# Expert results stored in sorted order and fetched by row number, in place of a scatter to token order

## What is computed

```python
x = x + gnn(layernorm(x), adj, W, a)         # attention inside each block of 128 tokens
x = x + ffn(layernorm(x), gate_w, gate_b, w1, w2, w3)

# gnn, for each block
Wh = h @ W.T; e = leaky_relu((Wh @ a1)[:, None] + (Wh @ a2)[None, :])
out = softmax(where(adj > 0, e, -9e15)) @ Wh

# ffn: 16 experts, hidden 256, each token goes to its best two
probs = softmax(x @ gate_w + gate_b); top2 = top_k(probs, 2); gates = top2 / sum(top2)
out = sum over the two of  gate * ((silu(x @ w1[e]) * (x @ w2[e])) @ w3[e])
```

## Time and profile before

| | |
|---|---|
| timed, median of 3 | 522.09 us (520.78 to 522.9) |
| profiled execution, span from first to last instruction | 661.6 us |
| its own time | recorded only as that span |
| TensorE busy | 409.6 us, 62% |
| VectorE busy | 250.0 us, 38% |
| GpSimd busy | 316.4 us, 48% |
| mean granted TensorE clock | 0.804 |

### The profile page before, as it was taken

One profiled execution on the slowest core, in us unless ns is written; L12 is line 12 of the kernel. 1 busy time (PEld: TensorE's weight loads), 2 busy tenths in 40 slices (PEclk: granted clock), 3 DMA queues, 4 the chain that ended last, 5 costly groups with the idle time before them and its releaser, 6 DMA issues.

```text
span 661.6 us, 10734 instructions
## 1 busy us (share of the span) xinstructions
PE 409.6 (62%) x2857; PEld 372.2 (56%) x2860; DVE 250.0 (38%) x915; ACT 194.3 (29%) x516; POOL 316.4 (48%) x340
## 2 busy tenths in 40 slices
PE   3787863675520313773563788697877888878700
PEld 2576753554520313672462778687777888777700
DVE  2898898654356001120110122221221234343328
ACT  1687760454310101220120133322322333232200
POOL 3123321657477771557357444444444445643530
PEclk9999995679555575985677689898997989997855
DMA  3999992696131312351342455555555579777347
GB/s 105 225 234 240 248 255 63 148 185 159 58 126 52 100 68 95 133 196 68 119 155 80 159 195 210 177 198 194 188 191 196 191 259 312 246 255 263 130 167 242
DMA packets 126058, 113.88 MB, mean 172 GB/s; under 512 B 10704, under 2 KB 100944, under 8 KB 126032
## 3 DMA queue, kind: packets, MB, share of 16 engines
q1 hardware_dynamic: 116816, 94.64, 49.2%
q0 software_dynamic: 9216, 18.96, 8.2%
HBM read 33.72 MB, written 33.70 MB: 102 GB/s over the span
## 4 chain that ended last, share of the span: by engine, by line
PE 36%; issue 23%; DVE 14%; another core or an unknown queue 9%; DMA 7%; ACT 5%; POOL 2%; SPq 2%; DVEq 1%; ACTq 0%; POOLq 0%
PE bank L475 21%; PE bank L484 8%; PE bank L384 4%; DMA shared<-in_adj_dram 3%; DMA w_t<-W 2%; DVE prob L815 2%; ACT em L590 2%; DVE stats L635 1%; DVE h L645 1%; DVE X L698 1%; ACT h L536 1%; POOL token_rows L924 1%; PE bank L428 1%; PE bank L430 1%
## 5 line engine op out<-in xcount | busy, mean ns | idle before, releaser
L924 POOL DMA_INDIRECT token_rows<-shared,DEST x160 | 154.1, 963 | 179.4 <-ACT shared L596 127.4
L475 PE MATMUL bank<-xT,w_t 128*128 128x128 f32 x1280 | 196.2, 298 | 49.2 <-issue 27.5
L475 PEld LDWEIGHTS bank<-xT,w_t 128*128 128x128 f32 x1280 | 176.0, 211 | 56.0 <-issue 41.0
L815 DVE TENSOR_TENSOR prob<-em,bank 128x256 f32<-128x256 f32 x160 | 66.6, 421 | 316.9 <-ACT em L590 214.0
L916 POOL DMA_INDIRECT sorted_rows<-H,ROW x128 | 125.6, 981 | 53.0 <-issue 37.4
L484 PE MATMUL bank<-W,prob 128*128 x640 | 109.9, 298 | 61.5 <-DVE prob L815 33.4
L590 ACT ACTIVATE em<-bank 128x256 f32<-128x256 f32 x160 | 60.6, 387 | 275.2 <-PE bank L475 135.6
L484 PEld LDWEIGHTS bank<-W,prob 128*128 128x128 f32 x640 | 92.8, 209 | 70.6 <-issue 70.5
L904 POOL TENSOR_TENSOR rstd<-var_eps,half_neg 128x4 f32<-128x4 f32 x32 | 32.3, 1022 | 82.8 <-DVE var_eps L651 82.8
L384 PE MATMUL bank<-ident,xs_t 128*128 128x128 f32 x160 | 29.3, 306 | 27.5 <-DMA xs_t<-sorted_rows 20.2
L584 ACT ACTIVATE xT<-bank 128x512 f32<-128x512 f32 x40 | 23.8, 596 | 55.4 <-issue 31.3
(11 more groups left out here) (100 smaller groups left out, 372.8 us busy)
## 6 DMA issues: line engine op xcount, KB each, us to landing
w_t<-W SPq DMA_DIRECT2D x160, 256.0 KB
sorted_rows<-zeros SPq DMA_DIRECT2D x16, 645.0 KB, 8.0
xs_t<-sorted_rows SPq DMA_DIRECT2D x40, 258.0 KB
W<-in_L_ffn_w_dram SPq DMA_DIRECT2D x48, 128.0 KB
X<-in_x_dram SPq DMA_DIRECT2D x16, 256.0 KB
shared<-in_adj_dram SPq DMA_DIRECT2D x16, 256.0 KB
H<-h SPq DMA_DIRECT2D x16, 256.0 KB
hT<-token_rows SPq DMA_DIRECT2D x6, 512.0 KB
```

The lines of the kernel that those rows point to most:

```text
L475: ins = nc.tensor.matmul(H[k][:, m * P:(m + 1) * P], w_t[:, k, m * P:(m + 1) * P], xT[:, par, k * P:(k + 1) * P], start=True, stop=True)
L815: V.tensor_tensor(hidT[:, k, :], sil[:, k % 2, :], H[k][:, HC * P:2 * HC * P], ALU.mult).then_inc(hid_ready, 1)
L924: pool.indirect_dma_start(ys[q // QS], bass.IndirectOffsetOnAxis(ap=DEST[:, q * QT + k:q * QT + k + 1], axis=0), yo[:, q % YB, k * D:(k + ...
```

## The change

- The destination word is gone: rows are 128 words, 512 bytes. With it go both iotas, the wait for the scatters of choice 0 and `keep_dest`.
- `send` is gone. SyncE stores the results of quad q as they are, in sorted order, with one plain DMA of 256 KB (`store_rows`).
- GpSimd issues all 64 scatters of segment 1 in one stretch. Then it fetches: `fetch(j, b)` brings the two results of each of a group's four tiles by eight indirect DMAs of 128 rows, with the row numbers in `ROW`. The fetches of segment 0 are paced by `hid_ready`, one for each tile of quads 22 to 37; those of segment 1 start when all stores of segment 1 have landed.
- `load_results` is gone; the groups of segment 0 are added beside quads 25, 27, ..., 39.
- The zero fill writes the same region with 5,120 contiguous bytes from each partition in place of ten rows of 516.
- `yo` has four slots in place of eight, and a few loops are written out.

```diff
-    DW = D + 1
-    YB = 8
+    YB = 4
     CG = TS // QT
-    CB = NQ - 3 * CG // 2
+    C0 = QS + 2
+    CB = C0 + 2
...
-            n = q - CB
-            return 2 * (n // 3) + n % 3 if n >= 0 and n % 3 < 2 else None
+            n = q - (C0 + 3)
+            return n // 2 if n >= 0 and n % 2 == 0 else None
...
-                sp.dma_start(xs[s][bass.ds(c * ZC * P, ZC * P), :].rearrange("(t p) n -> p t n", p=P), zeros[:]).then_inc(zeroed[s], 16)
+                sp.dma_start(xs[s][bass.ds(c * ZC * P, ZC * P), :].rearrange("(p t) n -> p (t n)", p=P), zeros[:]).then_inc(zeroed[s], 16)
...
-            def load_results(s, j, b, after=None):
...
+            def store_rows(s, q, slot):
+                sp.wait_ge(yo_ready, q + 1)
+                sp.dma_start(ys[s][bass.ds((q - s * QS) * QT * P, QT * P), :].rearrange("(t p) d -> p t d", p=P),
+                             yo[:, slot, :].rearrange("p (t d) -> p t d", d=D)).then_inc(y_sent[slot], 16)
...
+            def step(n, s, odd, stored, slot):
+                load_quad(s, n + 2, odd)
+                load_up(n + 1)
+                if stored is not None:
+                    store_rows(stored, n - 1, slot)
...
-            def keep_dest(q, par):
...
-                if n == TS:
-                    pool.wait_ge(scattered[s], 16 * TS)
-                    g.iota(H2[:, s * TS:(s + 1) * TS, D].bitcast(I32), pattern=[[2 * P, TS]], base=NT * P + 1,
-                           channel_multiplier=2).then_inc(dest_steps, 1)
...
-            def send(q):
-                pool.wait_ge(dest_ready, q + 1)
-                pool.wait_ge(yo_ready, q + 1)
...
+            def fetch(j, b, after=None):
                 for k in range(QT):
+                    for c in range(2):
+                        if after is not None:
+                            pool.wait_ge(hid_ready, after + 2 * k + c)
+                        t = j * QT + k
+                        pool.indirect_dma_start(got[b][:, k, c, :], None, ys[t // TS],
+                                                bass.IndirectOffsetOnAxis(ap=ROW[:, t // TS, c, t % TS:t % TS + 1], axis=0))\
+                            .then_inc(y_in[b], 16)
...
-            AHEAD, EACH = 26, 5
...
+            for m in range(2 * TS):
+                scatter(1, m)
+            for b in range(YB):
+                pool.wait_ge(y_sent[b], stored_before(0, b))
+            for j in range(CG):
+                if j >= 2:
+                    pool.wait_ge(res_ready, j - 1)
+                fetch(j, j % 2, C0 * QT + 2 * QT * j + 1)
+            for b in range(YB):
+                pool.wait_ge(y_sent[b], stored_before(1, b))
+            for j in range(CG, 2 * CG):
...
+                fetch(j, j % 4)
```

More of the change, by code:

```diff
@@ L333, in _ @@
             load_quad(0, 1, 1)
[L334 to L337, removed]
+            def step(n, s, odd, stored, slot):
[3 more added lines that the diff above has]
+                    store_rows(stored, n - 1, slot)
+            for n in range(2):
+                step(n, 0, n % 2, 0 if n else None, (n - 1) % YB)
+            with sp.Fori(0, (QS - 4) // YB) as r:
+                n = r * YB + 2
+                for k in range(YB):
+                    step(n + k, 0, k % 2, 0, (k + 1) % YB)
@@ L338, in _ @@
             sp.wait_ge(eid_ready, NSEG)
             sp.wait_ge(scattered[1], 16 * 2 * TS)
[L340 to L347, removed]
-                j = group_beside(n - 1)
[L349 to L366, removed]
+            for n in range(QS - 2, QS + 2):
+                step(n, 1, n % 2, (n - 1) // QS, (n - 1) % YB)
@@ new lines, in _ @@
+            for n in range(QS + 2, NQ - 2):
+                step(n, 1, n % 2, 1, (n - 1) % YB)
+                j = group_beside(n - 1)
+                if j is not None:
+                    store_group(j, j % 2)
+            load_up(NQ - 1)
+            store_rows(1, NQ - 3, (NQ - 3) % YB)
+            j = group_beside(NQ - 3)
+            if j is not None:
+                store_group(j, j % 2)
+            for n in range(NQ - 2, NQ):
+                store_rows(1, n, n % YB)
+                j = group_beside(n)
+                if j is not None:
+                    store_group(j, j % 2)
@@ L367, in _ @@
+            for j in range(CG, 2 * CG):
+                store_group(j, j % 4)
             for b in range(4):
@@ L867, in _ @@
-            for b in range(4):
-                combine(CG + b, b, seg0[b] + 16, seg0[b] or None)
-            with dve.Fori(0, (CG - 4) // 4) as r:
-                for b in range(4):
-                    combine(r * 4 + (CG + 4 + b), b, r * 16 + (seg0[b] + 32), r * 16 + (seg0[b] + 16))
+                    add_first(j, j % 2, 2 * QT * 16 * (j // 2 + 1))
+            if group_beside(NQ - 1) is not None:
+                j = group_beside(NQ - 1)
+                add_second(j, j % 2, 16 * (j // 2))
@@ L874, in _ @@
+            for j in range(CG, 2 * CG):
+                b = j % 4
+                before_b = CG // 2 if b < 2 else 0
+                add_first(j, b, 2 * QT * 16 * (before_b + (j - CG) // 4 + 1))
+                add_second(j, b, 16 * (before_b + (j - CG) // 4))
         @block.gpsimd
```

87 lines of the change are left out of this document (27 added, 60 removed).

## The result

The changed kernel takes 553.83 us (median of 4 runs, 553.26 to 555.3) where the kernel before takes 522.5 us (4 runs, 520.78 to 523.28) on the same chip: a ratio of 1.0601, with a 95% interval of 1.0574 to 1.0628. It is 31 us slower. My prediction said 566 us, with a range of 536 to 590.

What follows compares the result with a forecast made beforehand. It took VectorE to bound half one, GpSimd's scatters the start of half two, TensorE the quads, then a matmul-free tail. Terms +56.6 - 3.5 - 5.2 - 4 = +43.9 us on 522.09 gave 566 us, range 536 to 590.

Steps and rivals of the forecast that it cites:

- The tail: From the last copy to the end: 64 fetches at 1.264 us make it 89.9 us, a term of +56.6 us.
- The estimate by the Trainium skill's fit: Fetches in the tail: 2.15 us each by the skill's formula, 138 us in all, giving 622 us.
- The choice wait: GpSimd's gap between the scatters of choice 0 and 1 goes: -3.5 us in segment 0, nothing in segment 1.
- The zero fill: Half one: fewer, longer runs relieve the DMA engines and end VectorE's wait for `adj`, -5.2 us.
- The quads: Half two's quads: neither GpSimd nor SyncE sets their pace; only -4 us is won, from TensorE's wait for `w_t`.
- The -4 us for `w_t`: Quads: 64 KB fetches replace 512 KB loads ahead of weight copies, saving 4 of TensorE's 6.6 us wait.
- the store: SyncE's queue in the quads: one issue of about 0.5 us each, put at 0, up to 20 us if uncovered.
- The pauses: First ten quads of the profile: 84 us lost while GpSimd streams indirect DMAs; timed runs were read as having few.
- The rival of the halted quads: Segment 1's unbroken row of 64 scatters halts the quads in timed runs: 48 us lost, 614 us, 4 in 100.
- The quads are freed: Quads without bursts of sends: ScalarE and VectorE answer sooner, 56 us won over 40 quads, 510 us, 5 in 100.
- its milder form: Part of the quads' gain, or a fetch down to 0.96 us, gives 530 to 552 us, 17 in 100.
- the signs named for "wrong": Profile: fetches stepping 2 us or more, quads 10 to 21 below 6.8 us, stores then `w_t` waits, first-quad pauses gone.

Runs made afterwards that it cites:

- e6: Changed kernel with the wait between the scatters of choice 0 and 1 put back in both segments, without iotas: 651.95 us, where the kernel before took 657.59.
- e1: Kernel before with only the zero fill changed, to 5,160 contiguous bytes from each partition: 519.86 us against 525.91, ratio 0.9899.
- b0: Kernel before, unchanged, profiled a second time: 526.45 us, span 524.5, in a series where it took 525.91 us.
- e2: Changed kernel with only the zero fill put back to ten rows of 512 bytes from each partition: 553.38 us, ratio 1.0543 to the kernel before.
- e8: Kernel before with 20 memsets, one ahead of each quad's sends of segment 0: 548.98 us, ratio 1.0459, +24.2 us to before.
- e10: Kernel before with segment 0's results stored by SyncE, not sent; its groups add wrong rows with the same work: 509.21 us, ratio 0.9696, -15.6 us.

## Why the prediction came out as it did

It was 12 us too high, with the sign and the main term as measured: the tail is +52.2 us between the two spans. All the rest is -24.3, where the prediction had -12.7. By its own steps:

- **The tail.** Predicted at 89.9 us from the end of the last copy; measured 552.4 - 462.67 = 89.7 us: 3.25 us until the first fetch (2.7 predicted), 64 fetches to 545.63, 79.7 us (80.9), and 6.8 us behind them (6.3). Taking the sends' step for an operation that the trace didn't have was right, 1.250 us against 1.264, and so was the order in which fetches are bound by issue and not by landing. The estimate by the Trainium skill's fit ("DMA: Bandwidth & Descriptors", "Anatomy of one DMA"), 2.15 us each and 622 us in all, is not what these DMAs do: 64 KB every 1.250 us. The term was +56.6 and came to +52.2, since the old tail is longer without pauses: nine sends start behind the end of the last copy there, six in the earlier trace rows.
- **The choice wait.** Predicted -3.5 us; in the second profile of before the gap is 2.66 us where 0.30 is usual, so -2.4. That is a reading of the trace: e6, which has this wait alone, fell among pauses, and no run isolates it. The whole stretch up to the first copy is 10.0 us shorter, 6.9 of them in e1 as well. GpSimd's row at the gap, in b0:

```profile
168.08 0.20 POOL L913 IOTA H<- 128x32 int32 x1 [1.96 <-DMA sorted_rows<-H,ROW]
168.78 0.98 POOL L916 DMA_INDIRECT sorted_rows<-H,ROW  x1 [0.51 <-POOL H L913]
```

- **The zero fill.** Predicted -5.2 us; e1 measures -5 to -6 us and VectorE's wait for `adj` from 20 to 95 us goes from 6.0 us to 0.3 in e1 and 1.1 in the changed kernel. The size was right by luck, since the reason was wrong: not the longer runs but the row of 516 bytes was the cost, as e2 shows. The change would have had this gain from its 512-byte rows alone.
- **The quads: the step that failed.** I wrote "Neither GpSimd nor SyncE sets the pace of a quad", and put the whole of this part at -4 us, for shorter loads in front of weight copies. It is -14.3 us. GpSimd did set the pace: 252 indirect DMAs of 1.264 us behind the last root are 318.5 us, whatever the quads do, and the last copy cannot come before the 220 up to the sends of quad 31 are through, with eight slots in `yo`; e8 and e10 show it from both sides. It did so through copies 13 to 18, not in each quad: up to copy 12 TensorE was busy 70.60 of 70.61 us. This could have been worked out from the rows at hand, with the step of the earlier trace rows and the counts of the order. Instead I read GpSimd's 129 us of idle time from quads that the pauses had stretched to 7.88 us, and carried that idle time over into runs that I knew to be 139.5 us shorter. The -4 us for `w_t` did come where `load_results` had stood (11.0 to 6.8 us in copies 27 to 39), but it was lost again elsewhere, for the whole wait goes from 11.0 to 12.2 us. The step behind that is the store, which was put at 0: with it TensorE waits 3.4 us for `w_t` in copies 0 to 12, where before had no such wait, and 2.0 us in copies 19 to 27, where fetches stand beside it as well.
- **The pauses.** I put them down to the profiled execution, with timed runs that "have few of them". That the terms then held as durations was right for this comparison; the cause was not. In some series all timed runs have the pauses as well. The rival of the halted quads (614 us) did not come about in the timed comparison, but e6 shows its mechanism where there are pauses.
- **Rivals.** "The quads are freed" was right in kind, and its milder form held the time nearly: 530 to 552 us was given, 553.8 came. Little more was to be won there: TensorE is busy 176.4 of 186 us from 254 to 440 us in the changed kernel. The forecast's own range of 552 to 582 us holds the time at its edge. Three of the signs named for "wrong" came: quads 10 to 21 take some 5.9 us each, below the 6.8, the pauses of the first quads are gone, and SyncE's stores are followed by short waits for `w_t`.

The three terms add up: tail -4.4 to the forecast, quads -10.3, half one -1.3, together -16, which is 43.9 - 27.9. The spans are of two series; by the timed medians of one series the difference is 31.3 us, and the miss 12.

## What to carry to other kernels

Before taking an engine for idle, multiply its instructions by their step from one to the next (here 1.264 us, not the 0.96 us of busy time), add them up over the stretch, and hold the sum against the stretch in a *timed* run; an idle time read from a profile that is a quarter longer than the timed runs is idle time of another kernel. Work moved off a pacing engine wins only down to the next bound (16 us in copies 12 to 19 here), but work moved behind the last matmul is paid in full (64 x 1.25 us here): in e10 SyncE's stores in place of segment 0's sends were worth 15.6 us (e10 leaves out segment 0's fetches), and the longer tail costs 52.2. And when an edit wins by a layout, test each size that it changes by itself: the 516-byte row was the cost, the 5 KB run was not.

## What was unexpected of the hardware

- The same kernel took 525 us in one series and 658 us in another on the same chip, on all its runs. In the latter, other engines stand for about 20 us at a time while GpSimd streams indirect DMAs, and with a memset and a wait after each third DMA most of this is gone (594 against 652 us). The cause is open.
- An indirect DMA of 128 rows steps at 1.25 to 1.26 us whether it scatters 516-byte rows, scatters 512-byte rows or fetches 512-byte rows by number.
- Zero rows of 516 bytes land in 7.9 us per DMA of 1,280 rows, rows of 512 bytes in 5.0.
- Beside fetches the quads of segment 1 alternate from about the 27th copy on: one of 5.8 us is followed by one of about 7.7, as the changed kernel's ScalarE shows. TensorE waited 8.7 us for `w_t` between 300 and 455 us; whether fetches or the adds' stores hold the copies up was not tested.

```profile
387.74 0.59 ACT L586 ACTIVATE shared<-bank 128x512 f32<-128x512 f32 x1
393.54 0.59 ACT L586 ACTIVATE shared<-bank 128x512 f32<-128x512 f32 x1
401.34 0.59 ACT L586 ACTIVATE shared<-bank 128x512 f32<-128x512 f32 x1
407.14 0.59 ACT L586 ACTIVATE shared<-bank 128x512 f32<-128x512 f32 x1
```
